# Expert stage of a two-layer attention and routing kernel: the first expert in two groups of 128 rows, gathers issued one half ahead of another, the flag formed at the third expert

## The reference

```python
route_prob = softmax(xf @ Ws + bs, axis=-1).T          # 8 experts x 2048 tokens
route_vals, routes = top_k(route_prob, 256)            # k = 2048 / 8
xin = xf[routes]                                       # 8 x 256 x 128
h = gelu(einsum('ekd,edf->ekf', xin, W1) + b1[:, None])  # F = 512
out = einsum('ekf,efd->ekd', h, W2) + b2[:, None]
out = out * route_vals[..., None]
final = zeros((N, D)).at[routes.reshape(-1)].add(out.reshape(-1, D))
```

## Time and profile before

| | us |
|---|---|
| median of 3 runs | 264.07 (263.54 to 264.34) |
| profiled execution, its own time | 264.77 |
| its span, from the first to the last instruction | 262.70 |
| PE busy in the span | 210.8 (80%) |
| DVE busy | 155.9 (59%) |
| ScalarE (ACT) busy | 87.5 (33%) |
| GpSimd (POOL) busy | 83.7 (32%) |
| 16 scatter instructions, L1632 | 25.4 |
| 16 gather instructions, L1623 | 16.7 |

### The profile page before, as it was taken

One profiled execution on the slowest core, in us unless ns is written; L12 is line 12 of the kernel. 1 busy time (PEld: TensorE's weight loads), 2 busy tenths in 40 slices (PEclk: granted clock), 3 DMA queues, 4 the chain that ended last, 5 costly groups with the idle time before them and its releaser, 6 DMA issues.

```text
span 262.7 us, 3477 instructions
## 1 busy us (share of the span) xinstructions
PE 210.8 (80%) x1203; PEld 122.6 (47%) x1212; DVE 155.9 (59%) x523; ACT 87.5 (33%) x183; POOL 83.7 (32%) x91
## 2 busy tenths in 40 slices
PE   1797589998799969989999988998897998676400
PEld 0543245335364545366635554653333796666400
DVE  5898837619859989386739665768899122011100
ACT  3241046352433543155402323226710355050200
POOL 1348507000106011101110321300006678885454
PEclk9999999999999999999999999999999999797955
DMA  7600111001100007931100101200001223332222
GB/s 203 176 9 23 45 47 50 20 2 50 30 1 4 0 0 243 331 109 45 41 0 5 40 0 41 85 13 31 0 2 32 53 27 46 43 42 31 24 24 20
DMA packets 15190, 13.04 MB, mean 50 GB/s; under 512 B 3520, under 2 KB 12161, under 8 KB 15169
## 3 DMA queue, kind: packets, MB, share of 16 engines
q1 hardware_dynamic: 11440, 10.17, 12.5%
q0 software_dynamic: 3008, 2.31, 6.5%
q10 hardware_dynamic: 721, 0.30, 0.4%
HBM read 7.99 MB, written 3.21 MB: 43 GB/s over the span
## 4 chain that ended last, share of the span: by engine, by line
DVE 34%; PE 34%; POOL 11%; issue 7%; DMA 6%; ACT 3%; another core or an unknown queue 2%; POOLq 1%; DVEq 0%; ACTq 0%
PE psum L884 7%; POOL out L1632 6%; DVE rden L1260 5%; DVE mrow L1239 5%; DVE xn L1192 4%; PE psum L802 4%; DMA out<-pT,idx 3%; DVE stats L1183 3%; DVE pT L1401 2%; POOL pT L1623 2%; DMA pT<-gather_rows,idx 2%; PE psum L807 2%; PE psum L866 2%; POOL rstd L1563 2%; PE psum L840 2%
## 5 line engine op out<-in xcount | busy, mean ns | idle before, releaser
L802 PE MATMUL psum<-c 128*128 128x512 bf16 x183 | 44.7, 379 | 0.5
L699 ACT ACTIVATE pT<-psum 103x512 f32<-103x512 f32 (+1 forms) x48 | 28.4, 597 | 45.0 <-PE psum L868 44.9
L1562 POOL TENSOR_SCALAR ve<-mv 128x4 f32<-128x4 f32 (+1 forms) x19 | 4.3, 229 | 95.3 <-DVE mv L1186 95.2
L1239 DVE TENSOR_REDUCE mrow<-psum 128x4 bf16<-128x308 f32 x64 | 27.4, 470 | 5.1 <-PE psum L840 4.6
L1632 POOL DMA_INDIRECT out<-pT,idx x16 | 25.4, 1586 | 14.2 <-DMA out<-pT,idx 5.8
L1623 POOL DMA_INDIRECT pT<-gather_rows,idx x16 | 16.7, 1044 | 31.7 <-DVE idx L1461 27.1
L802 PEld LDWEIGHTS psum<-c 128*128 128x128 bf16 x192 | 18.4, 99 | 17.4 <-issue 0.6
L1469 DVE TENSOR_TENSOR pT<-psum,b_rows 128x256 f32<-128x256 f32 x8 | 3.4, 425 | 34.3 <-PE psum L1143 24.1
L840 PE MATMUL psum<-k_stack,q_stack 128*128 128x308 f16 x64 | 16.7, 298 | 7.2 <-DVE mrow L1239 6.8
L773 ACT ACTIVATE pT<-psum,b 128x256 f32<-128x256 f32 x32 | 13.6, 474 | 18.5 <-PE psum L1128 18.5
L1143 PE MATMUL psum<-w,pT 128*128 128x128 f32 x128 | 19.0, 309 | 0.8 <-ACT pT L773 0.8
(11 more groups left out here) (179 smaller groups left out, 352.8 us busy)
## 6 DMA issues: line engine op xcount, KB each, us to landing
w<-in_L_ffn_W SPq DMA_DIRECT2D x16, 256.0 KB, 5.9
gather_rows<-xrow SPq DMA_DIRECT2D x4, 272.0 KB, 2.1
x<-in_x SPq DMA_DIRECT2D x4, 256.0 KB, 4.4
out<-res SPq DMA_DIRECT2D x4, 256.0 KB, 2.0
q_stack<-q_hi SPq DMA_DIRECT2D x24, 32.0 KB, 1.8
q_stack<-q_lo SPq DMA_DIRECT2D x24, 32.0 KB, 1.9
b_rows<-in_L_ffn_b SPq DMA_DIRECT2D x1, 512.0 KB, 3.9
pT<-gather_rows,idx POOLq DMA_INDIRECT x16
```

Source lines behind the costliest of these rows:

```text
L699: nc.scalar.activation(pT[0:n, b % 2, s, :], ST_ps[s % 2][0:n, :], ACT.Exp).then_inc(exp_done, 1)
L802: pe.matmul(bank[b][:, :], ident16, c16[:, 0:4 * P], start=True, stop=True)
L1239: dve.tensor_reduce(mrow[:, b % 2, j, g * GH:(g + 1) * GH], S_ps[u % 2][:, 0:GK].rearrange("p (h k) -> p h k", h=GH), X, ALU.max).then_inc ...
```

## The change

- The unit of the expert stage becomes a group of rows: expert 0 has two groups of 128 rows, every other expert one of 256, nine in all (`GROUPS`, `NG`). PE, ScalarE and DVE loop over groups, with buffers and banks by the group's number. The first gather gets a semaphore of its own (`got_first`).
- POOL issues gathers and scatters by halves. Ahead of the first scatter stand five gather instructions: both halves of experts 0 and 1 and the first of expert 2. Behind the scatter of e follow the second half of e + 2 and the first half of e + 3. The first scatter of expert 0 waits for group 0 alone, the second for group 1.
- The 19 checks move on DVE from ahead of the stage to behind group 1, the flag's instruction to behind group 2 (expert 1). PE's product for the flag and its wait for the flag stand ahead of the second product of group 3 (expert 2).
- Two semaphores of the start (`w_k4_done`, `w_q4_done`) become one, `w_4_done`, counted to 1 and 2.

The position of `rows_T` of the next group ahead of the second product of this one is as before. The diff, cut to its core:

```diff
-LEAD = 4
+GROUPS = ((0, 0, 1), (0, 1, 2)) + tuple((e, 0, SH) for e in range(1, E))
+NG = len(GROUPS)
...
             def experts(again):          # ScalarE
 
-                for e in range(E):
-                    n = again * E + e
+                for k, (e, h0, h1) in enumerate(GROUPS):
+                    n, rows = again * NG + k, slice(h0 * P, h1 * P)
                     act.wait_ge(xinT_ps_done, n + 1)
-                    nc.scalar.copy(xinT[:, e % 2, :], bank[e % 2][:, 0:CAP]).then_inc(xinT_done, 1)
+                    nc.scalar.copy(xinT[:, k % 2, rows], bank[k % 2][:, rows]).then_inc(xinT_done, 1)
...
-            def rows_T(again, e):
-                n = again * E + e
-                pe.wait_ge(got[e], 16 * SH * (again + 1))
-                if e >= 2:
+            def rows_T(again, k):
+                n, (e, h0, h1) = again * NG + k, GROUPS[k]
+                if h1 == 1:
+                    pe.wait_ge(got_first, 16 * (again + 1))
+                else:
+                    pe.wait_ge(got[e], 16 * (again + 1) * (h1 - h0))
+                if k >= 2:
                     pe.wait_ge(xinT_done, n - 1)
                 else:
                     pe.wait_ge(idx_done, 2 * again + 2)
...
-                    if n == 0:
+                    if k + 1 < NG:
+                        rows_T(again, k + 1)
+                    if n >= 2:
+                        pe.wait_ge(y_done, n - 1)
+                    if n == 3:
                         pe.wait_ge(suspect_done, 1)
                         pe.matmul(flag_ps, ones16[:, 0:1], suspect16[:], start=True, stop=True).then_inc(flag_ps_done, 1)
-                    if e + 1 < E:
-                        rows_T(again, e + 1)
-                    if n == 1:
                         pe.wait_ge(flag_done, 1)
-                    if n >= 2:
-                        pe.wait_ge(y_done, n - 1)
-                    for h in range(SH):
+                    for h in range(h0, h1):
                         for c in range(FC):
-                            if h == 0:
+                            if h == h0:
                                 pe.wait_ge(gelu_done, n * FC + c + 1)
...
+                        if not again and k == 1:
+                            suspects()
+                        if not again and k == 2:
+                            dve.wait_ge(flag_ps_done, 1)
+                            dve.tensor_scalar(flag[:], flag_ps, 0.5, None, ALU.is_gt).then_inc(flag_done, 1)
...
-            def scatter(again, e):
+            def scatter(again, e, h):
                 n = again * E + e
-                pool.wait_ge(y_done, n + 1)
+                pool.wait_ge(y_done, again * NG + (h + 1 if e == 0 else e + 2))
                 if n >= 1:
                     pool.wait_ge(out_add, 16 * SH * n)
...
                     if e == 0:
-                        for ahead in range(LEAD):
-                            gather(again, ahead)
-                    scatter(again, e)
-                    if e + LEAD < E:
-                        gather(again, e + LEAD)
+                        for ahead in range(2):
+                            for h in range(SH):
+                                gather(again, ahead, h)
+                        gather(again, 2, 0)
+                    for h in range(SH):
+                        scatter(again, e, h)
+                    if e + 2 < E:
+                        gather(again, e + 2, 1)
+                    if e + 3 < E:
+                        gather(again, e + 3, 0)
```

More of the change, by code:

```diff
@@ L239, in program @@
         rows_out = [sem(f"rows_out{b}") for b in range(B)]
-        got = [sem(f"got{e}") for e in range(E)]
+        got_first, got = sem("got_first"), [sem(f"got{e}") for e in range(E)]
         ones_set, ctxT_ps_done, ctxT_done = sem("ones_set"), sem("ctxT_ps_done"), sem("ctxT_done")
-        kT_ps_done, kT_done, w_k4_done, w_q4_done = (sem(n) for n in ("kT_ps_done", "kT_done", "w_k4_done", "w_q4_done"))
+        kT_ps_done, kT_done, w_4_done = (sem(n) for n in ("kT_ps_done", "kT_done", "w_4_done"))
         k4_ps_done, k_hi_done, k_lo_done, k_stack_done = (sem(n) for n in ("k4_ps_done", "k_hi_done", "k_lo_done", "k_stack_done"))
@@ L772, in experts @@
                         act.wait_ge(h_ps_done, n * FC + c + 1)
-                        nc.scalar.activation(hg[:, e % 2, c, :], bank[2 + c][:, 0:CAP], ACT.Gelu_apprx_tanh,
+                        nc.scalar.activation(hg[:, k % 2, c, rows], bank[2 + c][:, rows], ACT.Gelu_apprx_tanh,
                                              bias=b1[:, e * FC + c:e * FC + c + 1]).then_inc(gelu_done, 1)
@@ L1114, in rows_T @@
                     pe.wait_ge(idx_done, 2 * again + 2)
-                for h in range(SH):
-                    ins = pe.transpose(bank[e % 2][:, h * P:(h + 1) * P], xin[:, e, h, 0:D], ident)
+                for h in range(h0, h1):
+                    ins = pe.transpose(bank[k % 2][:, h * P:(h + 1) * P], xin[:, e, h, 0:D], ident)
                 ins.then_inc(xinT_ps_done, 1)
@@ L1465, in experts @@
                 def experts(again):
[L1467 to L1471, removed]
-                                          ALU.mult).then_inc(y_done, 1)
+                    for k, (e, h0, h1) in enumerate(GROUPS):
+                        hs, shape = slice(h0, h1), [P, h1 - h0, D]
+                        dve.wait_ge(y_ps_done, again * NG + k + 1)
+                        settle(dve.tensor_tensor(y[:, e, hs], bank[6 + k % 2][:, h0 * P:h1 * P].rearrange("p (h d) -> p h d", d=D),
+                                                 b2_rows[:, e, :].unsqueeze(1).broadcast_to(shape), ALU.add))
+                        dve.tensor_tensor(y[:, e, hs], y[:, e, hs], xin[:, e, hs, D + e].unsqueeze(2).broadcast_to(shape),
+                                          ALU.mult).then_inc(y_done, 1)
+                        if not again and k == 1:
[3 more added lines that the diff above has]
+                            dve.tensor_scalar(flag[:], flag_ps, 0.5, None, ALU.is_gt).then_inc(flag_done, 1)
```

75 lines of the change are left out of this document (36 added, 39 removed).

## The result

The changed kernel takes 291.69 us (median of 4 runs, 291.26 to 291.86) against 263.92 (4 runs, 263.54 to 264.34): a ratio of 1.105, 95% interval 1.103 to 1.107. So it is slower by 27.8 us. The forecast was 289.3 in a range of 280.5 to 294.

The account below looks back on a forecast made before the run. Expert stage bounds, POOL's 6.55 us per expert becoming a PE-POOL loop: second scatter 207.8, expert 1 217.2, five 11.4 rounds plus flag 0.4 to 274.6, landing 6.2, end 7.04: span 287.9, forecast 289.3 us (280.5 to 294).

Parts of the forecast that it names:

- five rounds to expert 6, with the flag: POOL's scatters of experts 2 to 6: five rounds of 11.4 us each, plus 0.4 us once for the flag.
- landing wait: Expert 7's scatter waits for the landing of the pair before: one wait of 6.2 us.
- last pair to the end: From the start of the last scatter pair to the end of the span: 7.04 us, as before.
- Front: Start of expert stage: first group needs one gather; first scatter at 205.6 instead of 210.94, second at 207.8.
- 2.05 us hold: Unexplained wait at the front: expert 0's second product issued by 207.62, DVE started at 209.77; about 2.1 us.
- DVE and flag: 19 checks moved behind group 1 cost nothing, 0.7 us if uncovered; flag costs 0.4 us once on PE's path.
- The loop: Experts 1 to 6: y waits behind next transposes, whose gather follows the previous scatter; 11.4 us per round against POOL's 6.55.
- transposes to y: PE transposes through second product and DVE: 3.14 us at full clock, 4.78 or 4.34 slower; 4.55 taken.
- Two of the signs: Expected in the profile after: scatter pairs 10 to 11.7 us apart; POOL idle 4 to 5 us before each pair.
- A: Same loop with PE at full clock: 9.98 us per round, time 280.8, or 279 with front at lower bound; chance 0.18.
- C: Loop doesn't close, POOL's 6.55 us per expert holds: time 260.1; chance 0.05.
- B: Same loop, front not earlier and every round slow: time 296, or 292.7 with the 2.1 us alone; chance 0.13.

Follow-up runs that it names:

- e4: Kernel before with only POOL's gather and scatter order of the changed kernel; no groups, checks and flag as before: 294.72 us, ratio 1.115.
- e2: Changed kernel with six gather instructions ahead (experts 0, 1, 2 whole) and both halves of expert e + 3 behind each scatter pair: 261.68 us, ratio 0.992.
- e1: Changed kernel with PE's transposes of the next group moved behind the second product of this one, POOL's order kept: 261.83 us, ratio 0.992.
- e9: Changed kernel with three gather instructions behind the first scatter pair and both halves of expert e + 3 behind each later pair: 263.69 us, ratio 1.007.
- e3: Changed kernel with small products that feed nothing added in PE's pauses (30, then 45 ahead of the waiting transposes): 281.57 us, ratio 1.066.
- e8: Changed kernel with the sixth gather between expert 0's two scatters, then both halves of expert e + 3 behind each pair: 260.50 us, ratio 0.986.
- e7: Kernel before, unchanged, profiled once more: 263.78 us.
- e5: Changed kernel with POOL's order of before (experts 0 to 3 whole ahead, expert e + 4 behind each scatter pair): 263.23 us, ratio 0.995.
- e6: Kernel before with only the 19 checks, the flag and PE's product for it moved later: 262.67 us, ratio 0.995.
- e10: Kernel before, without groups, with POOL's order of e8 (five gathers, first scatter, sixth gather, second scatter): 266.12 us, ratio 1.015.
- e11: e8 repeated unchanged, beside a kernel before of 261.38 us: 260.30 us, ratio 0.996.
- e12: Kernel before, unchanged, a third profile, on another chip: 262.26 us.

## Why the prediction was right

Counted from the first gather, step by step (forecast; measured in the changed kernel):

| step | forecast | measured |
|---|---|---|
| first scatter | 7.4 | 7.1 |
| second scatter | 9.6 | 9.5 |
| scatter of expert 1 | 19.1 | 19.5 |
| five rounds to expert 6, with the flag | 57.4 | 59.5 |
| landing wait | 6.2 | 6.5 |
| last pair to the end | 7.0 | 7.0 |
| sum | 89.7 | 92.5 |

**Front.** Right, as to the size too; the transpose came when the warm-up products ended, 200.18. The groups did what they are for (first scatter at 7.1, against 10.7 without them in e4). The 2.05 us hold in the kernel before stands in its time and is no part of the changed kernel.

**DVE and flag.** The checks ran from 206.15 to 210.50, hidden as forecast, y of expert 1 being first touched at 215.28. The loop itself gave them that cover; in e2, where it is open, they cost 0.44 together with the hold. The round with the flag was 0.47 longer than the mean of the others, for 0.4 forecast.

**The loop.** Right in kind: e1, e2, e4 and e9 show it from four sides. The mis-sized term is transposes to y. I took 4.55, the mean of two rows of before, "the two that came out of a wait for a gather". There were four such rows: the transposes at 218.85 and 232.12 had waited too, 0.64 and 1.07 us, and ran at full clock; the two taken were those with the longest waits, 2.47 and 2.67 us. Measured were 5.01 to 5.03 (5.45 with the flag). Even the slower of the two, 4.78 (rows 4 and 6), had its transposes still at full clock (0.52 us for the pair, 0.69 after), since there the clock fell just as PE came back: the granted clock was 1.00 from 225.00 to 225.70 and 0.50 behind it. In the changed kernel, after pauses of 3.9 to 6.0 us, all of this work was at 1.2 GHz. Over six rounds that term is 2.9 us too small; the sum is 2.8 short, since the small differences of the other terms nearly cancel. The first gather, 1.2 us earlier in this execution, hid part of it in the span (289.5 for 287.9). That was luck. Two of the signs came out larger than named: pairs up to 12.3 us apart for 10 to 11.7, and POOL idle 5.5 to 6.9 us for 4 to 5.

**Readings that were off.** The prediction lets all three pairs behind the last gather of the kernel before wait for a landing. The first of them waited for DVE's y, so the loop's chain shows there already:

```profile
243.06 1.56 POOL L1632 DMA_INDIRECT out<-pT,idx  x1 [2.39 <-DVE pT L1471]
```

The two real landing waits were 6.75 and 5.85, not 6.2 each; 6.48 came. In A, the time with the front at its lower bound is 279.9, not 279. In C, the four periods to 239.3 are counted from 213.1, so C carries the checks' 0.7. None of this moves the forecast by more than 0.1 us.

**The rules of the Trainium skill.** The windows show 0.50 to 0.55 over transposes and second product of every round. By the Trainium skill's "TensorE: Matmul & The Clock Gate" (HAM oscillation), a loop whose transfers outlast its work starts each round at the slow clock; the trace agrees. The prediction priced that rule at 11.62 us per round, from rows, and took 11.4; measured were 11.75 to 11.86 in the rounds behind the first without the flag. That page's remark on weight loads pulled ahead in PE's queue (Part 1, engine queue depths) doesn't reach past a waiting instruction here: in e1 the same instructions in the other order took 30 us less. The 2.16 us estimated from "DMA: Bandwidth & Descriptors" of the Trainium skill (Anatomy of one DMA) were 2.64 to 2.76 in the changed kernel, from the gather instruction's start to PE's.

**Rivals.** A (281) is what e3 measured, with fillers: 281.57. B was half right: every round was slow, as it says, but its late front didn't come, there being no hold with five gathers ahead. The measured 291.69 stands 2.4 above the forecast, on B's side. C was what the change may look like from POOL's side alone; with the loop open in every round, e8 comes to 260.50 for C's 260.1.

## What to carry to other kernels

Where an engine takes its instructions in order, an instruction that waits for a transfer holds everything queued behind it. So a transfer has to be issued early enough for the first instruction that stands behind its wait, not only for the one that uses its data: here the second product of e stood behind the transposes of e + 1. Before making a queue shorter, write down for each instruction what stands behind it on its engine, and follow who waits for that back to the issuer: if it comes round within one period, the period becomes the latency of the chain. And price such a loop with the clock that PE has after the pause that the loop itself creates.

## What the runs showed of the hardware that was not expected

PE's results were held back at the front in five of the six profiles with more than five gathers queued ahead: 2.05 us (kernel before), about 2.0 (e7), 2.6 (e5) and 0.8 (e6) with eight, 1.3 with six (e2); ScalarE and DVE then started 0.03 us apart (209.74 and 209.77 in the kernel before) on products that PE had issued up to 2 us earlier. In the eight profiles with five ahead (changed kernel, e1, e3, e4, e8, e9, e10, e11) DVE started at most 0.35 us after PE had issued. There was no hold in e12 either, with eight ahead on another chip, so e9, e10 and e11, from chips on which the kernel before has medians of 261.4 and 261.6, say little of the number ahead; the other five do. What holds the results isn't shown: neither the groups nor the place of the flag's product is needed for it (e6, e5). It may hang on the chip or on the execution: one profile without it doesn't part the two.

Indirect transfers cost POOL the same whatever they wait for: 0.99 to 1.20 us for a gather of 128 rows, 1.55 to 1.76 for an adding scatter, and about 0.30 between two.
